# Record fields of a graph kernel turned by transposing transfers, head checks and loads moved, a third one-hot buffer

## The reference

```python
h = jnp.maximum(_layernorm(x, axis=-1), 0.0)
x = x + segment_sum(edge_weight[:, None] * (sigmoid(h @ Wg + bg) * (h @ W0))[src], dst)       # layer 0
h = ...; x = x + einsum('nc,oc->no', segment_sum(h[src], dst), W1) + b1                       # layer 1
h = ...; x = x + (concat([h, segment_sum(concat([h[src], h[dst]]) @ Wm + bm, dst)]) @ Wu + bu)  # layer 2
h = ...; x = x + relu(batchnorm(D_inv * segment_sum((B_inv * segment_sum(hW3[row], col))[col], row) + b3))  # layer 3
```

## Time and profile before

| what | value |
|---|---|
| median of 3 runs | 2613.72 us (2612.69 to 2618.68) |
| the profiled execution, its own time | 2625.16 us |
| its span | 2623.4 us |
| PE, PEld busy | 2342.7 us (89%), 2004.2 us (76%) |
| DVE, ACT busy | 1601.8 us (61%), 1235.6 us (47%) |
| POOL busy | 38.0 us (1%) |

### The profile page before, as it was taken

One profiled execution on the slowest core, in us unless ns is written; L12 is line 12 of the kernel. 1 busy time (PEld: TensorE's weight loads), 2 busy tenths in 40 slices (PEclk: granted clock), 3 DMA queues, 4 the chain that ended last, 5 costly groups with the idle time before them and its releaser, 6 DMA issues. The chain is left out here.

```text
span 2623.4 us, 71483 instructions
## 1 busy us (share of the span) xinstructions
PE 2342.7 (89%) x27976; PEld 2004.2 (76%) x27976; DVE 1601.8 (61%) x3701; ACT 1235.6 (47%) x2695; POOL 38.0 (1%) x46
## 2 busy tenths in 40 slices
PE   2689999999989998999938999899998999999996
PEld 2468787778777777777837888788887888887884
DVE  6689999999999998999962333234333222121224
ACT  2578787778777777777732222222222000011113
POOL 3100000000000000000000000000000000000000
PEclk9889999999999999999979999999998999999996
DMA  6279999999999999999999999899997999999994
GB/s 188 65 143 204 217 212 216 204 204 208 219 181 207 202 203 195 204 203 199 202 230 233 283 284 282 228 261 258 253 257 202 290 289 290 272 256 248 266 268 114
DMA packets 1595771, 586.11 MB, mean 223 GB/s; under 512 B 951206, under 2 KB 1592234, under 8 KB 1595351
## 3 DMA queue, kind: packets, MB, share of 16 engines
q1 hardware_dynamic: 1592219, 574.02, 99.5%
q0 software_dynamic: 1600, 4.92, 0.6%
q10 hardware_dynamic: 1660, 3.20, 0.5%
HBM read 255.26 MB, written 89.20 MB: 131 GB/s over the span
## 5 line engine op out<-in xcount | busy, mean ns | idle before, releaser
L1159 ACT CAST stage<-ps 128x784 f16<-128x784 f32 x784 | 654.4, 835 | 97.2 <-DMA counts_by_source<-stage 61.9
L617 PE MATMUL ps<-Ha,a_tiles 128*128 128x258 f16 x4802 | 548.2, 274 | 46.3 <-ACT Ha L1206 38.9
L617 PEld LDWEIGHTS ps<-Ha,a_tiles 128*128 128x128 f16 x4802 | 470.0, 98 | 116.8 <-ACT Ha L1206 39.1
L570 PE MATMUL ps<-hot_c,hot_r 128*128 128x98 f16 x3136 | 508.7, 212 | 11.6 <-DVE hot_c L868 5.9
L571 PE MATMUL ps<-hot_c,hot_r 128*128 128x98 f16 x3136 | 502.8, 210 | 0.0
L572 PE MATMUL ps<-hot_c,hot_r 128*128 128x98 f16 x3136 | 501.5, 210 | 0.0
L1144 ACT CAST stage<-ps 128x392 f16<-128x392 f32 x784 | 397.3, 507 | 169.2 <-PE ps L553 169.2
L545 PE MATMUL ps<-g_in,wt 128*128 128x128 f16 x2401 | 430.7, 222 | 44.2 <-DVE X L880 33.0
L546 PE MATMUL ps<-g_in,wt 128*128 128x128 f16 x2401 | 427.8, 221 | 0.0
L547 PE MATMUL ps<-g_in,wt 128*128 128x128 f16 x2401 | 427.6, 221 | 0.0
L880 DVE SCALAR_TENSOR_TENSOR X<-ps,X 128x512 f32<-128x512 f32 (+1 forms) x637 | 390.4, 649 | 15.5 <-PE ps L547 15.5
(11 more groups left out here) (199 smaller groups left out, 2084.0 us busy)
## 6 DMA issues: line engine op xcount, KB each, us to landing
a_tiles<-counts_by_source SPq DMA_DIRECT2D x147, 1600.0 KB, 9.2
counts_by_source<-stage SPq DMA_DIRECT2D x49, 1600.0 KB, 8.0
gated_parts<-G SPq DMA_DIRECT2D x7, 448.0 KB, 3.0
g_in<-gated_parts SPq DMA_DIRECT2D x98, 32.0 KB, 2.9
out_x<-X SPq DMA_DIRECT2D x6, 512.0 KB
edge_table<-tab SPq DMA_DIRECT2D x1, 2448.0 KB, 9.8
wt<-stage SPq DMA_TRANSPOSE x98, 10.8
dst_run<-in_dst SPq DMA_DIRECT2D x1, 612.4 KB
```

Of the source, the lines that this page charges most:

```text
L570: mm(into(0), rows_, codes(0), start=v == 0, stop=True, skip_group_check=True)
L617: last = mm(ps[:, c % 2, 0:PARTS], a_slot(ph, c, i), moving[:, i], start=i == 0, stop=i == TILES - 1)
L1159: a.copy(stage[:, b, 0:2, 0:TILES, u * SET_COLS:(u + 1) * SET_COLS], of).then_inc(s("hi_done"), 1)
```

## The change

1. **Turning.** DVE now makes the fields in float16 (`pre` with two key fields, `pre_w` with the two halves of the weight), of batches of five groups (five batches instead of seven). SP turns them by two transposing transfers per batch (`turn_keys`): the keys straight into `meta` (now laid out by group), the weights into `turned_w`. POOL interleaves `turned_w` into `meta_w` (`interleave`). PE's transposes, ACT's copies to `meta` and DVE's two operations from PSUM are gone.
2. **Head.** The four long passes of the checks move ahead of DVE's wait for `x`; `x` is loaded on SP's queue behind the runs, and the small weights on ACT's queue.
3. **Third buffer.** `hot_r` and `hot_c` have three slots; a hot waits for the one three back.

```diff
 HALF = HOT // 2
 PAIRS = HOT // 2
 WEIGHTS = 2
+HOT_SLOTS = 3
 ALIGN = 16
 SAMPLES = 102
 RUN = ALIGN * SAMPLES
@@ -42,7 +43,7 @@
 WIDE = P + 2
 CHUNKS = -(-EDGES // P)
 PADDED = CHUNKS * P
-BATCH = 4
+BATCH = 5
 BATCHES = -(-GROUPS // BATCH)
 LOT_BANKS = (3, 6, 7)
 THREE = -(-TILES // 3)
...
             run_in(w_run, edge_weight, 0, "w_in", 2)
             run_in(src_run, src, 0, "src_in", 3)
-            for to, of in ((w0g[:, 0:P], w0), (w0g[:, P:P + 1], wg0), (w3s[:], w3), (w_h[:, 0], wu[0:P]),
...
-                sp.dma_start(to, of).then_inc(s("weights_in"), 16)
-            sp.wait_ge(s("x_zero"), 2)
-            sp.dma_start(hrows[0:TILES - 1, :], hyper[0:(TILES - 1) * P].rearrange("(i p) -> i p", p=P)).then_inc(s("weights_in"), 16)
-            sp.dma_start(hrows[TILES - 1:TILES, 0:LAST], vec(hyper[(TILES - 1) * P:NODES])).then_inc(s("weights_in"), 16)
-
+            sp.dma_start(X[:, 0:TILES - 1, :], x[0:(TILES - 1) * P].rearrange("(i p) f -> p i f", p=P)).then_inc(s("x_in"), 16)
+            sp.wait_ge(s("x_zero"), 1)
+            sp.dma_start(X[0:LAST, TILES - 1, :], x[(TILES - 1) * P:NODES]).then_inc(s("x_in"), 16)
             sp.wait_ge(s("tab_keys"), 1)
             sp.wait_ge(s("tab_src"), 1)
             sp.dma_start(table.rearrange("(p n) a -> p (n a)", p=P), tab[:].rearrange("p n a b -> p (n a b)")).then_inc(s("table_in"), 16)
 
-            for c in range(SET):
+            def turn_keys(m):
+
+                lot = batch(m)
+                sp.wait_ge(s("pre"), m + 1)
+                sp.dma_start_transpose(meta[:, lot.start:lot.stop].rearrange("e n a q b -> e (n a) (q b)"),
+                                       pre[:].rearrange("q n a e -> q (n a e)")).then_inc(s("keys_in"), 16)
+                if m:
+                    sp.wait_ge(s("meta_w"), m)
+                sp.dma_start_transpose(turned_w[:].rearrange("e a (n q) -> e (a n) q", q=P),
+                                       pre_w[:].rearrange("q a n e -> q (a n e)")).then_inc(s("weights_turned"), 16)
+
+            def store_gated(c):
+
                 sp.wait_ge(s("g_parts"), c + 1)
                 tiles = slice(c * SET, (c + 1) * SET)
                 sp.dma_start(g_dram[tiles].rearrange("i p n -> p i n"), G[:, tiles].rearrange("p i a f -> p i (a f)")).then_inc(s("g_stored"), 16)
+
+            for m in range(3):
+                turn_keys(m)
+            store_gated(0)
+            turn_keys(3)
+            store_gated(1)
+            store_gated(2)
+            turn_keys(4)
+            for c in range(3, SET):
+                store_gated(c)
 
...
-            for c in range(SET):
+            def interleave(m):
+
+                pool.wait_ge(s("weights_turned"), 16 * (m + 1))
+                lot = batch(m)
+                pairs = meta_w[:, lot.start * P // 2:lot.stop * P // 2].rearrange("p q a b -> p a q b")
+                g.tensor_copy(pairs, turned_w[:].rearrange("p a (q b) -> p a q b", b=2)).then_inc(s("meta_w"), 1)
+
+            def high_parts(c):
+
                 pool.wait_ge(s("h0_done"), (c + 1) * SET)
                 g.tensor_copy(G[:, c * SET:(c + 1) * SET, 0], H0[:, c * SET:(c + 1) * SET]).then_inc(s("g_high"), 1)
+
+            interleave(0)
+            interleave(1)
+            high_parts(0)
+            high_parts(1)
+            interleave(2)
+            high_parts(2)
+            interleave(3)
+            high_parts(3)
+            high_parts(4)
+            interleave(4)
+            high_parts(5)
+            high_parts(6)
...
-                m, at_step = divmod(j - 9, 6)
-                if m in range(BATCHES) and at_step == 4:
-                    pe.wait_ge(s("pre"), m + 1)
-                    if m:
-                        pe.wait_ge(s("meta_keys"), m)
-                        pe.wait_ge(s("meta_w"), m)
-                    else:
-                        pe.wait_ge(s("flag"), 1)
-                    for u in range(len(batch(m))):
-                        for a in range(3):
-                            last = tr(ps[:, a, u * P:(u + 1) * P], pre[:, a, u], ident[:])
-                    last.then_inc(s("turned"), 1)
-
             def general_sum(ph):
...
+            v.tensor_tensor(viol[:], dst_run[:, 0:RUN], dst_run[:, 1:RUN + 1], ALU.is_gt)
+            v.tensor_reduce(w_lim[:, 0:1], w_run[:], AX.X, ALU.max)
+            ch(v.tensor_reduce(w_lim[:, 1:2], w_run[:], AX.X, ALU.min))
+            v.tensor_reduce(bad[:, 0:1], viol[:], AX.X, ALU.max)
             dve.wait_ge(s("x_in"), 32)
...
                 if j == 1:
-                    done["viol"] = ch.mark(v.tensor_tensor(viol[:], dst_run[:, 0:RUN], dst_run[:, 1:RUN + 1], ALU.is_gt))
-                if j == 2:
-                    v.tensor_reduce(w_lim[:, 0:1], w_run[:], AX.X, ALU.max)
+                    done["limits"] = ch.mark(v.tensor_reduce(bad[:, 6:7], hist[:], AX.X, ALU.max))
                 if j == 3:
-                    v.tensor_reduce(w_lim[:, 1:2], w_run[:], AX.X, ALU.min)
-                    done["limits"] = ch.mark(v.tensor_reduce(bad[:, 6:7], hist[:], AX.X, ALU.max))
-                if j == 4:
-                    ch.wait(done["viol"])
-                    v.tensor_reduce(bad[:, 0:1], viol[:], AX.X, ALU.max)
-                if j == 5:
                     ch.wait(done["limits"])
                     v.tensor_scalar(bad[:, 1:2], bad[:, 6:7], float(FITS), None, ALU.is_gt)
                     v.tensor_scalar(bad[:, 2:3], w_lim[:, 0:1], W_MAX, None, ALU.is_gt)
                     v.tensor_scalar(bad[:, 3:4], w_lim[:, 1:2], -W_MAX, None, ALU.is_lt)
                     v.tensor_scalar(bad[:, 4:5], w_lim[:, 2:3], W0_MAX, None, ALU.is_gt)
                     done["tests"] = ch.mark(v.tensor_scalar(bad[:, 5:6], w_lim[:, 3:4], -W0_MAX, None, ALU.is_lt))
-                if j == 7:
+                if j == 5:
                     ch.wait(done["tests"])
                     v.tensor_reduce(bad[:, 7:8], bad[:, 0:6], AX.X, ALU.add).then_inc(s("bad"), 1)
-                if j == 12:
+                if j == 10:
                     dve.wait_ge(s("bad_ps"), 1)
                     v.tensor_copy(flag[:], ps[:, 0, 0:1]).then_inc(s("flag"), 1)
...
@@ -775,29 +803,19 @@
                 if at_step == 1:
                     ch.wait(done["src"])
                     if m:
-                        dve.wait_ge(s("turned"), m)
-                    v.tensor_copy(pre[:, 0, 0:n], ri[:, 0, 0:n])
-                    done["codes"] = ch.mark(v.scalar_tensor_tensor(four(pre[:, 1, 0:n]), field(1), float(TILES), four(ri[:, 1, 0:n]), ALU.mult, ALU.add))
+                        dve.wait_ge(s("keys_in"), 16 * m)
+                    v.tensor_copy(pre[:, 0:n, 0], ri[:, 0, 0:n])
+                    done["codes"] = ch.mark(v.scalar_tensor_tensor(four(code[:, 0:n]), field(1), float(TILES), four(ri[:, 1, 0:n]), ALU.mult, ALU.add))
                 if at_step == 2:
                     ch.wait(done["codes"])
-                    done["based"] = ch.mark(v.tensor_tensor(pre[:, 1, 0:n], pre[:, 1, 0:n], basef[:, lot.start:lot.stop].unsqueeze(2).to_broadcast([P, n, P]), ALU.add))
-                    v.tensor_copy(four(pre[:, 2, 0:n]), field(2).bitcast(F32))
+                    v.tensor_tensor(code[:, 0:n], code[:, 0:n], basef[:, lot.start:lot.stop].unsqueeze(2).to_broadcast([P, n, P]), ALU.add)
+                    if m:
+                        dve.wait_ge(s("weights_turned"), 16 * m)
+                    done["high"] = ch.mark(v.tensor_scalar(four(pre_w[:, 0]), field(2).bitcast(F32), W_UP, None, ALU.mult))
                 if at_step == 3:
-                    ch.wait(done["based"])
-                    flat = pre[:, 1, 0:n].rearrange("p n e -> p (n e)")
-                    v.tensor_scalar(flat, flat, -1.0, 255.0, ALU.max, ALU.min).then_inc(s("pre"), 1)
-
-            def edge_weights(m, at_step):
-
-                lot, n = batch(m), len(batch(m))
-                pairs = slice(lot.start * P // 2, lot.stop * P // 2)
-                of = ps[:, 2, 0:n * P].rearrange("p (n b) -> p n b", b=2)
-                if at_step == 0:
-                    dve.wait_ge(s("turned"), m + 1)
-                    done["high"] = ch.mark(v.tensor_scalar(meta_w[:, pairs, 0], of, W_UP, None, ALU.mult))
-                if at_step == 1:
                     ch.wait(done["high"])
-                    v.scalar_tensor_tensor(meta_w[:, pairs, 1], of, W_UP, meta_w[:, pairs, 0], ALU.mult, ALU.subtract).then_inc(s("meta_w"), 1)
+                    v.scalar_tensor_tensor(four(pre_w[:, 1]), field(2).bitcast(F32), W_UP, four(pre_w[:, 0]), ALU.mult, ALU.subtract)
+                    v.tensor_scalar(pre[:, 0:n, 1], code[:, 0:n], -1.0, 255.0, ALU.max, ALU.min).then_inc(s("pre"), 1)
 
             for j in range(TILES + SET + 3):
                 if j < TILES:
...
             def layers(general):
 
-                def hots(j, h):
-                    b = h % 2
+                def hots(j, k, c, h):
+                    b = hot_at(c, h)
                     hot = j * TILE_HOTS + h
```

(14 more changed lines are left out.)

59 lines of the change are left out of this document (27 added, 32 removed).

## The result

| | before | changed |
|---|---|---|
| median, us | 2618.47 (2609.14 to 2623.11, 11 runs) | 2606.45 (2598.01 to 2609.79, 10 runs; an eleventh of 5831.16 left out) |
| ratio | | 0.9958, 95% interval 0.9944 to 0.9972 |
| profiled execution: span, us | 2623.4 | 2606.2 |
| first hot, us | 131.66 | 131.26 |
| first three tiles, us | 66.89 | 65.42 |

The kernel is 0.42% faster by the ratio of the runs, 11 us (the medians are 12.0 us apart), where 0.83% was forecast (2613.72 to 2592 us); the time lies inside the range. Stage by stage the forecast was less right than its sum: in the two profiled executions the head gave 0.4 us where 11 were forecast, the steady tiles 18.9 where 9 were, and the rest took 3.6 us more. These two executions are 17.2 us apart, more than the medians: the profiled one of before, 2625.16 us, lies above all eleven timed runs.

What follows compares the result with a forecast made beforehand. DVE was taken as the build's tightest engine, 23.2 us a tile. Head -11, first tiles -2 and steady tiles -9 made -22 us, from the median 2613.72 to 2592 us; range 2566 to 2610 us.

Steps and rivals of the forecast that it cites:

- the head: Stage before the first hot: forecast 11 us shorter, between 0 and 15, from 14.7 us less 3.5 us.
- the steady tiles: The build's last 46 tiles: third buffer saves 0.2 us a tile, 9 us, a third of the bound.
- the rest: The 1306.6 us behind the build, which the change does not touch: counted as unchanged.
- a phase that I can't explain: Head, 56.8 to 76.7 us: DVE waits 16.4 us on PE while POOL gathers; about 7 us if it recurs, half taken.
- The chain itself: Head after the gathers: transfers, interleaving copies, casts and G operations in sequence, build beginning near 117 us, 14.7 us earlier.
- rival D: Head: transposing pairs are dear, 18.9 us each if cost ignores size, three on the path; 2630 us, chance 0.08.
- the page's price: Head: skill page's 1309 ns per transposed block, 13.1 us for ten blocks, 26 us a pair; would give 2652 us.
- the first tiles: The build's first three tiles, idle 10.9 us: third buffer saves 2 us, between 0 and 7.
- The bound of 23.75 us a tile: Steady tiles: the stores' round trip of 47.5 us for two tiles limits the saving to 26 us.
- Rival B: Build: its waits go nearly all; head -14.7, first tiles -7, steady -26, giving 2566 us; chance 0.12.
- Rival C: Build: third buffer does nothing, since the adds wait for the same hot; head gives 7 us, 2607 us; chance 0.12.
- Rival E: Build: a hot is dearer with new key layout or third slot; 100 ns each gives 2631 us; chance 0.08.

Runs made afterwards that it cites:

- r10: The changed kernel with POOL's gathers in pieces (ten, then three of five), on the same chip as r11; 2596.85 us, one run.
- r11: The changed kernel itself, unaltered, timed beside r10 on the same chip; 2608.03 us, one run.
- r6: The changed kernel itself, timed again beside r9 on one chip; 2592.14 us, ratio 0.9912 to the kernel before.
- r9: The kernel before, unaltered, timed again on the same chip as r6; 2616.30 us, one run.
- e4: The changed kernel with the store of the counts issued ahead of a tile's two transposing transfers; 2621.25 us, ratio 1.0020 to the kernel before.
- e2: The kernel before with only the third hot slot added and the destinations' run moved in memory; 2606.50 us, ratio 0.9969.
- e5: The changed kernel with the four long passes of the limits back in the loop's steps 1 to 3, behind the wait for x; 2587.98 us, one run.
- e1: The changed kernel with the hots in two of the three slots; 2608.38 us, ratio 0.9982 to the kernel before.
- e7: The changed kernel with POOL's casts ahead of the late interleaving copies and two buffers for the turned weights; 2604.61 us, ratio 0.9951 to the kernel before.
- r5: The changed kernel itself, timed again on the same chip as e7; 2606.29 us, ratio 0.9955 to the kernel before.
- e6: The changed kernel with POOL's gathers in pieces, the first try of the edit in r10; 2593.84 us, ratio 0.9935 to the kernel before.
- r7: The changed kernel with POOL's gathers in pieces, as e6, on the same chip as r6; 2592.27 us, ratio 0.9908 to the kernel before.

## Why the prediction was half right

**The step that failed** is the one on "a phase that I can't explain": "If that lies in the gathers' traffic it goes on as before and is hidden behind the first interleaving copy ... I take half, 3.5 us". It went with the long row of gathers (r10 against r11), but it isn't hidden, and in place of 3.5 us it costs 14 us: the first hot at 131.3, 130.7 and 132.7 us with it, at 117.0 to 117.1 without. The working held a contradiction. It read from the earlier trace rows that 45 of 59 steps come after 76.67 us, so that the loop stands at step 14 there, and then started its chain with DVE "at step 26" when the gathers end. In the first profile of the changed kernel the loop stood at step 12 at 76.17 us; batch 0 was only written at 72.7 us (54.7 in r6) and batch 2 at 95.3 us (81.0 in r6), so that the whole chain ran some 14 us late. SP's rows for the keys of these two batches:

```profile
72.76 1.47 SPq L362 DMA_TRANSPOSE meta<-pre  x1
...
95.30 1.32 SPq L362 DMA_TRANSPOSE meta<-pre  x1
```

**The chain itself was right**, where the loop isn't held. In r6, in us:

| | forecast | measured |
|---|---|---|
| first interleaving copy ends | 74.4 | 74.6 |
| weights of batch 1 landed | 78.8 | about 78.0 |
| batch 2 written, turned | 81.0, 87.0 | 81.0, 86.7 |
| batch 3 written, turned | 90.2, 96.2 | 92.3, 97.3 |
| batch 4 written, turned | 105.6, 111.6 | about 107.0, 112.0 |
| first hot | 117 | 117.0 |

The rows, of SP, POOL and DVE:

```profile
81.06 1.32 SPq L362 DMA_TRANSPOSE meta<-pre  x1
82.42 1.59 SPq L366 DMA_TRANSPOSE turned_w<-pre_w  x1
...
92.29 1.34 SPq L362 DMA_TRANSPOSE meta<-pre  x1
93.68 1.51 SPq L366 DMA_TRANSPOSE turned_w<-pre_w  x1
```

```profile
73.33 1.26 POOL L483 COPY meta_w<-turned_w 128x1280 f16<-128x1280 f16 x1
78.05 1.58 POOL L483 COPY meta_w<-turned_w 128x1280 f16<-128x1280 f16 x1 [3.46 <-DMA turned_w<-pre_w]
79.57 2.40 POOL L488 CAST G<-H 128x896 f16<-128x896 f32 x2
86.75 2.04 POOL L483 COPY meta_w<-turned_w 128x1280 f16<-128x1280 f16 x1 [4.78 <-DMA turned_w<-pre_w]
```

```profile
87.80 1.67 DVE L811 TENSOR_TENSOR code<-code,basef 128x640 f32<-128x640 f32 x1
```

Ten blocks take 1.3 to 1.6 us to issue in these rows (1.6 forecast) and a pair lands in 5.7 us for batch 2 and in about 5.0 us for batches 3 and 4 (6.0 forecast), so rival D is out, and so is the page's price. The Trainium skill, "VectorE: DVE Perf Modes", the section on the three transpose paths, gives 1309 ns for one block; an estimate from it is 13.1 us for ten blocks, and this trace does not agree.

What the sum lacked is in the rows of POOL and DVE: a copy of 1.25 us takes 1.58 or 2.04 us beside DVE's work, and DVE's operations of 0.81 us took up to 1.67 us there, about 0.9 us on batch 2 and 1.6 us on batch 3; pairs that land up to 1 us sooner make up for part of it. DVE's row above shows how: the operation starts at 87.80 us and ends at 89.47, 0.7 us after POOL's copy ended at 88.79. The Trainium skill, "SBUF — State Buffer", in its section on SBUF's two sides, says that GpSimd and a DVE operation with two SBUF inputs (or in a two-port mode) hold a shared pair of ports in turn, each for its whole instruction; the trace agrees, since both are long only where they overlap.

A reading of the forecast was wrong beside this. It put five of a batch's operations at 0.49 us and three at 0.81, 4.9 us a batch. It is the other way round, three of the cheap kind (L801, L802, L814) and five of the dear, and the five batches cost DVE 30.6 us in r6 and 31.3 in the first profile, not 24.4: DVE's work in the head hardly shrank. The chain's times above came out all the same. (In the earlier trace rows DVE ends its adds at 510.76 us, not 510.66; nothing hangs on it.)

**Where that leaves the sum.** On chip A without a crawl the whole change is worth 0.88% (r6), and the 2592.14 us are the forecast's 2592; in the first timing and on chip C with it, 0.42 and 0.45%. That the forecast's number came true on chip A is in part luck, since two errors cancel there. Between the profiles of r9 and r6 the head gives 13.1 us (11 forecast), the first tiles 1.3 (2), the steady tiles 19.3 (9), and the rest takes 6.8 us more (0).

**The steady tiles** were under-sized: 0.2 us a tile forecast, 0.41 measured in the two first profiles, and 24.20 against 23.87 us as a mean over five profiles with two slots and fourteen with three (e4 left out), 0.33 us or 15 us in all. The mechanism was right: waits moved to the adds, ACT goes on waiting for the store. The size was taken as a third of the bound, after one long stall of which a slot gives back 1.3 us. In the first two profiles, of all waits of DVE for another engine there, those under 1 us fell from 19 (11.4 us) to 9 (4.6 us) and the longer ones from 11 (29.0 us) to 9 (19.4 us): the short ones, which the working didn't look at, gave 7 of these 16.5 us. The bound of 23.75 us a tile from the stores' round trip held: the lowest of the fourteen is 23.76. Against it stand layers 1 to 3, which were counted as unchanged: 1306.6 to 1310.2 us in the first two profiles, and 1307.3 to 1310.3 as means over four profiles of the kernel before (e2 among them) and fifteen of the changed kernel (variants among them, e4 left out). PE's wait for the transposed counts is the part that the lines show (9.4 us before, 12.0 here; 8.6 in r9, 13.9 in r6), and its cause stays open:

```profile
L649 PE MATMUL ps<-Hb,a_turned 128*128 128x258 f16 x2401 | 277.9, 274 | 14.3 <-DMA a_turned<-counts_by_source 12.0 <-ACT Hb L1250 2.2
```

**The other terms.** First tiles: 1.5 us, 2 forecast. `x` came at 27.93 us, 28 forecast, with the passes ahead of it; they are worth 1.5 us (e5). Rival B fell: DVE still idles 34 us. Rival C fell with e2. Rival E fell: a `hot_c` takes 554 ns, 556 before, and a steady tile's work of DVE is as before.

**Open.** The parts alone, 0.31% (e2) and 0.18% (e1), make 0.49%, and together they make 0.88% on the same chip (r6, 0.60 to 1.15%). Their own intervals (0.17 to 0.44, 0 to 0.37) leave room for this to be chance; no run tells. And what the crawl is. Shown is where it came: never on A and B, in fourteen profiles; on C and D in three of four, with one wait of its kind in the fourth, r10. Since C and D were used on one occasion each, the chip and how the program was loaded on it aren't told apart. That it needs a long unbroken row of gathers rests on one pair of profiles (r10, r11). It takes the form of late updates of PE's products, on which DVE and then ACT wait. Why it appears in one place and not in another no trace here tells.

## What to carry to other kernels

Before a new chain is laid through a stage, write down at which step each engine stands at the chain's first time, from a window that counts its instructions, and check it against the chain. A phase of waits without a releaser has to be priced for both cases, hidden and not; a cover that hides it before (here POOL's gathers ahead of the first `G`) may be what the change removes. And a gain in such a phase should be timed on more than one chip. Price DVE's and POOL's work where they overlap as one behind the other.

## What the runs showed of the hardware that was not expected

- On some chips, while POOL's queue issued a row of 25 indirect transfers, one each 1.25 us, the changed kernel's loop made only five to seven steps in 28 us (first profile, e7, r5, r11), against twenty in r6; with the row in pieces of ten and five there was one such wait, of 5.4 us (r10). PE's semaphore updates came 1.5 to 6.3 us behind the recorded ends of its products there, and 0.01 us behind elsewhere.
- A store of 1600 KB issued ahead of two transposing transfers delayed them from 10.8 to 13.3 us and cost 1.1% against the changed kernel on the same chip (1.0020 against 0.9912), though the store had been the transfer that was waited for (e4).
- A copy on GpSimd and operations of DVE that overlap slow one another: the copy from 1.25 to 1.58 and 2.04 us, DVE's operations from 0.81 to 1.67 us (r6). Beside three of POOL's instructions without a gap DVE's `G` operation of 1.08 us took 3.86 us (r10; 3.85 in e6 and r7), ending 0.9 us after the last of them.
